# Zeroing cut to 256 rows an expert, loads and reloads spread out, and the turns of retiring tiles queued a unit later

## Chip, cores and metric

One Trainium2 chip, all 8 cores, each running the same program on its own quarter of one of two sequences. The time is device microseconds of the slowest core. Engines: PE is TensorE, DVE VectorE, ACT ScalarE, POOL GpSimd, SP the engine that only issues DMAs. POOL's DMAs go through a software queue (q0), SP's through a hardware queue (q1), on the same 16 DMA engines.

## What is computed

The reference, cut to what matters (x is 2 x 8192 x 1024, f32; b is zero):

```
q, k, v = split(layernorm(x) @ W + b)
x = x + softmax(mask(q @ k.T / 32)) @ v              # causal, one head of 1024
y = layernorm(x); probs = softmax(y @ router_w)       # 8 experts
topw, topi = top_k(probs, 2)
routed = sum over the 2 experts of topw * (silu(y @ w1[e]) @ w2[e])
shared = sigmoid(y @ gate_w) * ((silu(y @ g) * (y @ u)) @ shared_down)
out = x + routed + shared
```

A core computes 2048 query rows (16 tiles of 128 rows) of its sequence against all 8192 keys and values that are not masked away, and then the experts for its 2048 tokens.

## The kernel before, in words

**Attention.** Q's and K's projections are folded into one matrix M. Own tiles are turned (transposed) and multiplied by M into QT, two tiles by one `project(p)`. The keys come in 8 blocks (kb) of 8 tiles of 128 rows; a tile is loaded (POOL), normed (DVE and ACT) to XN and turned by a DMA of SP to XT. The work goes by **units** x = (kb, t), own tile t against key block kb: 72 of them, 16 in block 0, then 14, 12, 10, 8, 6, 4, 2. The loop over x (line 887) issues for each unit: `qk(x)` (PE, L579), `av(x - 2)` (PE, L642, evicted by DVE at L653 or L655), a `project` if x is in `project_at` (line 854), `softmax(x)` (DVE reduce L597, ACT exp L609 into P, then SP's turn PT<-P, L626), the steps of retiring tiles, zeroing and loads, and some steps of the norm of the next block. Each engine and each DMA queue runs in the order of issue. So in program order the softmax of a unit comes behind the eviction of av(x - 2) on DVE, and PE can be more than a unit ahead of it. P has three buffers, PT two.

**Norm steps.** `ln_steps` (line 291) makes a list per block: statistics of tile i (`ln_stats`, DVE), norm of tile i - 1 (`ln_norm`, ACT), turn of tile i - 2 (`ln_turn`, SP, L288). The loop takes the next few of the list each unit. Own tiles 4 to 15 go in block 0, nine steps in units 0 and 1 and five in each later one. Key block 1 has its own list, its turns by hand, two in each of units 10 to 13 (line 931). Tiles 0 to 5 of block 1 are all loaded at unit 5 (line 915), V's weights WV in eight pieces in units 10 to 17 (line 908).

**Retiring tiles.** After the last key block of own tile t its O is finished in four steps. `retire_a` (line 684), at unit x0 = its last unit + 3 (18, 20, 23, 25 for tiles 0 to 3): O / sum into a P buffer (ACT, L689) and the turn QT<-P (SP, L691). `retire_b` at x0 + 2: times WV on PE (L703, then the bias, L706), plus x (DVE, L708), layernorm into xf (ACT, L725) and the turn QT<-xf (SP, L728). `retire_c` at x0 + 5: the router's logits (PE, L739) and top 2; tiles 0 to 9 are stored to R in DRAM by POOL, since their place is needed. `retire_d` at x0 + 6: the place of each token in its expert's rows (L782), and two indirect DMAs of POOL that scatter xf's rows to G. In one unit the order is d, c, b, a.

**Zeroing.** G holds CAP = 640 rows for each of 8 experts. Rows that no token takes must be finite, so `zero_part` (line 867) writes zeros to all of them beforehand: 16 parts of 320 rows (640 KB each), 6 before unit 0 and 2 in each of units 3 to 7, each pair behind a wait of POOL for qk of its unit.

**Experts.** A flag (line 963) tells whether an expert has over 640 tokens; then a dense path runs, which these inputs don't take. The other path (from line 1130): per expert the first product (L1160, 128 matmuls of 320 columns, ACT to hT), then five tiles of the second (L1185, 16 matmuls of 512 columns each), each copied by DVE (L1198) to one of three ys buffers and stored to Y by SP (L1200). Between these tiles the next expert's rows, five tiles in one buffer xn, are turned on PE (`turn_rows`, L989), and after the fourth SP loads the rows of the expert after that (`load_rows`, L982). POOL loads w1 and w2 of expert ex + 2 as soon as their buffers are read. After the first product of expert 0 `back` (line 1017) makes SP reload all ten O tiles from R (L1020). At the end the outputs are gathered by rows, the shared expert's last product is added (L1265), and O is stored.

Of the kernel before, what the change touches and what calls it, by code (L numbers as in the profile page):

```python
# [10 lines left out]
ALU = mybir.AluOpType  # L11
AX = mybir.AxisListType
# [6 lines left out]
EPS = 1e-5  # L19
CAP = 640  # L20


# [59 lines left out]
def build_program():  # L82
# [20 lines left out]
    G = dram("G", [7 * CAP + 2048, D], BF16, kind="Internal")  # L103
    R = dram("R", [10 * 128, D], kind="Internal")
    Y = dram("Y", [8 * CAP, D], kind="Internal")
    out = dram("out", [NT * 128, D], kind="ExternalOutput")
# [184 lines left out]
    def ln_steps(jobs):  # L291
        out_ = []
        for i in range(len(jobs) + 2):
            if i < len(jobs):
                out_.append(lambda i=i: ln_stats(jobs[i]))
            if 0 <= i - 1 < len(jobs):
                out_.append(lambda i=i: ln_norm(jobs[i - 1], False))
            if 0 <= i - 2 < len(jobs):
                out_.append(lambda i=i: ln_turn(jobs[i - 2]))
        return out_  # L300
# [383 lines left out]
    def retire_a(t):  # L684
        i = t % 2
        a = DVE.do(lambda e: e.reciprocal(invl[:, i:i + 1], den[:, t:t + 1]), den_tok[t],
                   ret[t - 2]["ab"] if t > 1 else None)
        p = p_next()
        ab = ACT.do(lambda e: e.activation(out=P[p][:], in_=O[t][:], func=AF.Identity, scale=invl[:, i:i + 1]),  # L689
                    a, o_half[t, 0], o_half[t, 1], p_free[p])  # L690
        k = SP.dma(lambda e: e.dma_start_transpose(qt_cols(t), P[p][:]), d_at[i], ab, qk_last[t])  # L691
        p_free[p] = k
        ret[t] = dict(ab=ab, at=k)

    def retire_b(t):
# [31 lines left out]
        rs_free[z] = a  # L727
        xf_turned[t] = SP.dma(lambda e: e.dma_start_transpose(qt_cols(t), xf[f][:]), d_xf[f], a, k)  # L728
        r["xf"] = a
# [121 lines left out]
    for j in range(9):  # L851
        last_steps += [lambda j=j: ln_stats(kv[1, j])] if j < 8 else []
        last_steps += [lambda j=j: ln_norm(kv[1, j - 1], False)] if j > 0 else []
    project_at = [1, 3, 4, 5, 7, 8, 9]
    steps = []
    retire_at = {}
    for t in range(NT):
        x0 = (18, 20, 23, 25)[t] if t < 4 else units.index((t // 2, t)) + 3
        retire_at.setdefault(x0, []).append((retire_a, t))
        retire_at.setdefault(x0 + 2, []).append((retire_b, t))  # L860
        retire_at.setdefault(x0 + 5, []).append((retire_c, t))
        retire_at.setdefault(x0 + 6, []).append((retire_d, t))
# [3 lines left out]

    def zero_part(i):
        zero_tok[0] = POOL.dma(lambda e: e.dma_start(
            out=G[i * CAP // 2:(i + 1) * CAP // 2, :].rearrange("(s p) d -> p s d", p=64),
            in_=zero[0:64, :].unsqueeze(1).broadcast_to([64, CAP // 128, 1024])), d_zero, k_zeroed)  # L870

# [11 lines left out]
    k_taken = [DVE.do(lambda e: e.tensor_copy(taken[:], e640[:]), k_e640)]  # L883
    for i in range(6):
        zero_part(i)
    x = 0
    while x < n_units or x <= max(retire_at):
# [12 lines left out]
        if x < n_units:  # L900
            softmax(x)
        for step, t in sorted(retire_at.get(x, []), key=lambda v: (retire_d, retire_c, retire_b, retire_a).index(v[0])):
            step(t)
        if 3 <= x < 8:
            POOL.wait(qk_tok[x])
            zero_part(2 * x)
            zero_part(2 * x + 1)
        if 10 <= x < 18:
            w = slice((x - 10) * 1024, (x - 9) * 1024)
            k_wv[0] = POOL.dma(lambda e, w=w: e.dma_start(out=WV[:, w], in_=wvh[:, w]), d_wv, proj_done[7])  # L910
        if x == 18:
            xr_free[0] = zero_tok[0]
            POOL.wait(own[3]["turned"])
            load_xr(0)
        if x == 5:
            for j in range(6):
                ln_load(kv[1, j], POOL)
        for fc, g in fillers.get(x, []):
            gate_up(fc, g)
        if x < n_units:  # L920
            if kb == 0:
# [4 lines left out]
                if x >= 7:  # L926
                    for s in last_steps[:5]:
                        s()
                    last_steps = last_steps[5:]
                if 10 <= x < 14:  # L930
                    ln_turn(kv[1, 2 * x - 20])
                    ln_turn(kv[1, 2 * x - 19])
            elif kb < NKB - 1:
# [18 lines left out]
        for fc in {68: [0], 69: [1], 70: [2], 71: [3], 73: [4], 75: [5], 77: [6], 79: [7]}.get(x, []):  # L952
# [6 lines left out]
    wv_done = ret[NT - 1]["wv"]  # L959

    a = DVE.do(lambda e: e.tensor_tensor(out=rk[:], in0=taken[:], in1=e640[:], op=ALU.subtract), k_taken[0], place_tok[0])
    a = DVE.do(lambda e: e.reduce_max(over, rk[:], axis=AX.X), a)
    k_flag = DVE.do(lambda e: e.tensor_scalar(out=flag[:], in0=over, scalar1=float(CAP), scalar2=None,
                                              op0=ALU.is_gt), a)
# [51 lines left out]
    n = gu_n[0]  # L1016
    def back(queue, turned, k, d_rb):

        for t in range(10):
            tok = queue.dma(lambda e, t=t: e.dma_start(out=O[t][:], in_=R[t * 128:(t + 1) * 128, :]), d_rb, k, *turned)  # L1020
        return {t: tok for t in range(10)}
# [14 lines left out]
    o_done = {}  # L1036
    o_back = back(DSP, xt_tok, gu_done[7], d_rb)
    DPE.wait(k_dw)
# [111 lines left out]
    for ex in range(8):  # L1150
# [4 lines left out]
        for fc in range(8):  # L1155
# [14 lines left out]
            h_ready.append(sp_free[2 * j])  # L1170
        if ex == 0:
            o_back = back(SSP, xt_tok, k1, d_rb)
        if ex + 2 < 8:
# [4 lines left out]
        for s in range(CAP // 128):  # L1178
# [23 lines left out]
            if ex < 7 and s < 4:  # L1202
# [6 lines left out]
                if s == 3 and ex < 6:  # L1209
                    rows_in = load_rows(SSP, ex + 2, rows_out)  # L1210
        if ex + 2 < 8:
            load_w2(ex + 2, k2)
# [163 lines left out]
```

How the kernel before makes its waits and increments, by code:

```python
    def wait(self, *tokens):  # L38
        for t in tokens:
            if t is None:
                continue
            sem, val = t
            if val <= 0 or self.passed.get(id(sem), 0) >= val:
                continue
            self.passed[id(sem)] = val
            self.q.append(lambda e, s=sem, v=val: e.wait_ge(s, v))
# [1 line left out]
    def do(self, fn, *tokens):  # L48
        self.wait(*tokens)
        self.n += 1
        self.q.append(lambda e, f=fn, s=self.sem: f(e).then_inc(s, 1))
        return (self.sem, self.n)
# [5 lines left out]
    def dma(self, fn, slot, *tokens):  # L58
        self.wait(*tokens)
        slot.n += 16
        self.q.append(lambda e, f=fn, s=slot.sem: f(e).then_inc(s, 16))
        return (slot.sem, slot.n)
# [1218 lines left out]
    def run(e, main, one, other):  # L1281
        for fn in main.q:
            fn(e)
        full = e.alloc_register("full")
        e.wait_ge(*k_flag)
        e.reg_load(full, flag[0:1, 0:1])
        with e.If_eq(full, 0):
            for fn in one.q:
                fn(e)
        with e.Else():
            for fn in other.q:
                fn(e)
```

## Time and profile before

| | us |
|---|---|
| median of 3 runs | 1317.23 (1314.55 to 1317.49) |
| the profiled execution | 1328.9 |
| its span, core 7 (the slowest) | 1327.4 |
| spans of the 8 cores | 1293.9 to 1327.4 |
| PE busy on core 7 | 1148.4 (87%) |
| DVE, ACT, POOL busy | 580.6, 463.9, 273.8 |
| granted TensorE clock, mean of core 7 | 0.942 |

The span runs from the first to the last instruction of a core. Busy times are of core 7, and so are all rows below unless said otherwise. PEclk is the granted TensorE clock as a share of 2.4 GHz; at 0.5 a matmul takes twice as long. DMA is the mean busy share of the core's 16 DMA engines. In the name of a line, out<-in are the program's tiles without their numbers; SPq is SP's issue of a DMA, whose own time is that of writing it to the queue, not of the transfer.

### The profile page before, as it was taken

The numbers are of one execution on the slowest core, as the hardware profiler recorded it, in microseconds if no ns is written. First come the engines' busy times: TensorE is split into PE (matmuls) and PEld (weight loads), VectorE is DVE, ScalarE is ACT, GpSimd is POOL, SyncE is SP. The second block draws the span as 40 slices with busy tenths as digits, with TensorE's granted clock in tenths as the row PEclk, the third lists the DMA queues.
The fourth block names the chain that finished last, engine by engine and source line by source line (L and its number), as shares of the span: only waits on it lengthen the run. The fifth ranks groups of instructions, "written<-read, shape, count | busy, mean of one in ns | idle before, by whom it ended". The sixth has DMA issues, their size and how long they took to land.

```text
span 1327.4 us, 18849 instructions; the slowest of 8 cores (1293.9 to 1327.4 us)
## 1 busy us (share of the span) xinstructions
PE 1148.4 (87%) x6360; PEld 583.2 (44%) x6360; DVE 580.6 (44%) x1274; ACT 463.9 (35%) x899; POOL 273.8 (21%) x447
## 2 busy tenths in 40 slices
PE   4888849699989998988876979799985999999897
PEld 1555526244434443433332324344552666665333
DVE  3555315346656665656565654411111111111376
ACT  0344304325443543545445534412321222222200
POOL 4301300101112021221121032350120222111251
PEclk8989969899989999999988979899997999999899
DMA  9987972947766765996959886497398999999687
GB/s 173 242 192 139 212 87 50 149 69 159 131 150 145 167 160 136 203 202 134 187 130 160 154 140 121 77 185 130 102 240 214 198 201 219 223 214 208 236 286 318
DMA packets 249692, 227.03 MB, mean 171 GB/s; under 512 B 186996, under 2 KB 193268, under 8 KB 249592
## 3 DMA queue, kind: packets, MB, share of 16 engines
q0 software_dynamic: 53552, 131.12, 46.2%
q1 hardware_dynamic: 196040, 94.65, 35.5%
q8 instruction: 54, 0.88, 0.3%
q14 instruction: 46, 0.38, 0.1%
HBM read 174.35 MB, written 53.48 MB: 172 GB/s over the span
## 4 chain that ended last, share of the span: by engine, by line
PE 51%; DMA 18%; DVE 11%; ACT 9%; issue 6%; SPq 2%; POOL 1%; another core or an unknown queue 1%; DVEq 0%; ACTq 0%; POOLq 0%
PE po L642 9%; PE po L1185 8%; PE sp L1160 8%; DMA PT<-P 7%; PE sp L827 7%; PE sp L579 6%; PE po L521 4%; PE po L703 4%; DMA xn<-G 3%; DVE per_unit L597 3%; DMA Y<-ys 2%; ACT P L609 2%; PE po L1265 2%; DMA WKT<-wkt 2%; SPq L288 2%
## 5 line engine op out<-in xcount | busy, mean ns | idle before, releaser
L642 PE MATMUL po<-XN,PT 128*128 128x512 bf16 x1064 | 256.8, 397 | 74.9 <-DMA PT<-P 57.0
L579 PE MATMUL sp<-XT,QT 128*128 128x512 bf16 x1064 | 244.5, 383 | 7.1 <-DMA XT<-XN 3.4
L642 PEld LDWEIGHTS po<-XN,PT 128*128 128x128 bf16 x1064 | 106.4, 101 | 217.9 <-issue 107.5
L579 PEld LDWEIGHTS sp<-XT,QT 128*128 128x128 bf16 x1064 | 102.5, 98 | 130.8 <-issue 15.3
L1198 DVE COPY ys<-po 128x1024 f32<-128x1024 f32 x35 | 42.9, 1225 | 239.7 <-PE po L1185 208.6
L827 PE MATMUL sp<-QT,WGU 128*128 128x512 bf16 x512 | 114.3, 383 | 8.4 <-DVE HB L842 8.4
L655 DVE SCALAR_TENSOR_TENSOR O<-O,per_unit,po 128x512 f32<-128x512 f32 x112 | 80.3, 742 | 46.5 <-PE po L642 43.2
L607 ACT ACTIVATE per_unit<-nm,s_q 128x1 f32<-128x1 f32 x72 | 21.2, 295 | 221.4 <-DVE nm L604 88.4
L1167 ACT ACTIVATE hT<-sp 128x640 bf16<-128x640 f32 x64 | 45.0, 703 | 122.4 <-PE sp L1160 110.6
L1185 PE MATMUL po<-SW,hT 128*128 128x512 bf16 x320 | 77.2, 399 | 10.4 <-ACT hT L1167 6.6
L597 DVE TENSOR_REDUCE per_unit<-sp 128x1 f32<-128x1024 f32 (+1 forms) x72 | 83.5, 1160 | 2.0 <-DVE sp L595 0.5
L609 ACT ACTIVATE P<-sp,per_unit 128x1024 bf16<-128x1024 f32 (+1 forms) x72 | 76.7, 1066 | 11.5 <-DMA QT<-P 0.9
L827 PEld LDWEIGHTS sp<-QT,WGU 128*128 128x128 bf16 x512 | 49.9, 99 | 68.5 <-issue 11.4
L703 PE MATMUL po<-WV,QT 128*128 128x512 bf16 x256 | 66.5, 407 | 15.5 <-DVE O L655 8.0
L69 POOL DMA_DIRECT2D xs<-xkv x56 | 30.2, 544 | 217.7 <-ACT XN L278 164.2
L521 PE MATMUL po<-XT,M 128*128 128x256 bf16 x512 | 63.2, 286 | 13.6 <-DVE QT L533 6.6
L1185 PE MATMUL po<-W,hT 128*128 128x512 bf16 x320 | 72.3, 379 | 0.0
L1160 PE MATMUL sp<-xt,W 128*128 128x320 bf16 x512 | 70.4, 299 | 1.5 <-ACT xt L994 1.5
L994 ACT ACTIVATE xt<-sp 128x1024 bf16<-128x1024 bf16 x35 | 35.0, 1022 | 102.3 <-PE sp L989 102.3
L1160 PE MATMUL sp<-xt,SW 128*128 128x320 bf16 x512 | 70.2, 299 | 0.0
L521 PEld LDWEIGHTS po<-XT,M 128*128 128x128 bf16 x512 | 52.0, 102 | 25.3 <-issue 15.7
L69 POOL DMA_DIRECT2D O<-xkv x68 | 36.8, 551 | 113.0 <-ACT mvr L263 56.8
(160 smaller groups left out, 1385.4 us busy)
## 6 DMA issues: line engine op xcount, KB each, us to landing
Y<-ys SPq DMA_DIRECT2D x40, 512.0 KB, 8.0
O<-xkv POOLq DMA_DIRECT2D x68, 256.0 KB, 8.5
xs<-xkv POOLq DMA_DIRECT2D x56, 256.0 KB
G<-zero POOLq DMA_DIRECT2D x16, 640.0 KB, 14.9
xn<-G SPq DMA_DIRECT2D x8, 1280.0 KB, 18.6
xr<-xkv POOLq DMA_DIRECT2D x16, 512.0 KB, 5.0
W<-w1p POOLq DMA_DIRECT2D x32, 256.0 KB, 14.3
W<-w2p POOLq DMA_DIRECT2D x32, 256.0 KB, 17.7
```

Source lines behind the costliest of these rows:

```text
L69: k = queue.dma(lambda e, i=i: e.dma_start(out=out[:, i * w:(i + 1) * w], in_=src[:, i * v:(i + 1) * v]), slot, *tokens)
L521: fn = lambda e, d1=d1, d2=d2, i=i: e.matmul(ring[i][:, 0:256], M[:, d1 * 1024 + d2 * 128:d1 * 1024 + d2 * 128 + 128], rhs(d1), start=(d1 ...
L579: fn = lambda e, d=d, h=h: e.matmul(sp[j][:, h * 512:h * 512 + 512], QT[:, d * 2048 + t * 128:d * 2048 + t * 128 + 128], xt_of(kb)[:, h * ...
L597: a = DVE.do(lambda e: e.reduce_max(lb[:, z:z + 1], sp[j][:, 0:n], axis=AX.X, negate=True), a)
L609: exp_tok[x] = ACT.do(lambda e: e.activation(out=P[p][:, 0:n], in_=sp[j][:, 0:n], func=AF.Exp, bias=ebias[:, z:z + 1], accum_out=lsum[:, z ...
L642: fn = lambda e, c=c, h=h, i=i: e.matmul(ring[i], PT[p][:, c * 128:c * 128 + 128], xn_at(kb, c)[:, h * 512:h * 512 + 512], start=(c == 0), ...
L655: ring_free[i] = DVE.do(lambda e, i=i, dst=dst: e.scalar_tensor_tensor(out=dst, in0=dst, scalar=corr[:, z:z + 1], in1=ring[i], op0=ALU.mul ...
L703: PE.quiet(lambda e, d=d, h=h, b=b: e.matmul(ring[b], QT[:, d * 2048 + t * 128:d * 2048 + t * 128 + 128], WV[:, d * 1024 + h * 512:d * 102 ...
L827: fn = lambda e, d=d, part=part: e.matmul(sp[j][:, part * 512:part * 512 + 512], WGU[fc][:, d * 256 + part * 128:d * 256 + part * 128 + 12 ...
L1160: fn = lambda e, d=d, h=h, fc=fc, i=i, j=j, xt_=xt_: e.matmul(sp[j][:, h * 512:h * 512 + H], SW1[i][:, d * 1024 + fc * 128:d * 1024 + fc * ...
L1167: sp_free[2 * j] = sp_free[2 * j + 1] = SACT.do(lambda e, fc=fc, j=j: e.activation(out=hT[:, fc * CAP:(fc + 1) * CAP].rearrange("p (h n) - ...
L1185: fn = lambda e, fc=fc, h=h, s=s, i=i, j=j: e.matmul(po[j][:, h * 512:h * 512 + 512], hT[:, fc * CAP + s * 128:fc * CAP + s * 128 + 128], ...
```

## The change

1. Zeroing: each expert's rows 384 to 639 only (MIN = 384), one part of 512 KB per expert: four before unit 0, one in each of units 5 to 8. Experts with under 384 tokens would leave rows unwritten, so the flag now sends them, too, to the dense path: it takes the largest (tokens - 512)^2 over the experts and compares it with 128^2.
2. Block 1's tiles 0 to 5 are loaded one in each of units 3 to 8, each behind POOL's wait for that unit's qk; WV in units 9 to 16; block 1's turns in units 9 to 15, one a unit but for two in unit 10.
3. Projections 2, 5, 6 and 7 run one unit earlier.
4. `ln_steps`: the turn of tile i - 3 instead of i - 2, for own tiles and key blocks 2 to 7.
5. Tiles 0 to 13: QT<-P is issued a unit after retire_a and QT<-xf a unit after retire_b; in such a unit the order is turn_a, d, c, turn_b, b, a, all behind PT<-P of the unit. retire_b and retire_c stay where they were. Tiles 14 and 15 keep their order.
6. The ten reloads from R go out in pairs at the end of experts 1 to 5 instead of all in expert 0.

```diff
 CAP = 640
+MIN = 384
...
         out_ = []
-        for i in range(len(jobs) + 2):
+        for i in range(len(jobs) + 3):
...
                 out_.append(lambda i=i: ln_norm(jobs[i - 1], False))
-            if 0 <= i - 2 < len(jobs):
-                out_.append(lambda i=i: ln_turn(jobs[i - 2]))
+            if 0 <= i - 3 < len(jobs):
+                out_.append(lambda i=i: ln_turn(jobs[i - 3]))
...
                     a, o_half[t, 0], o_half[t, 1], p_free[p])
-        k = SP.dma(lambda e: e.dma_start_transpose(qt_cols(t), P[p][:]), d_at[i], ab, qk_last[t])
-        p_free[p] = k
-        ret[t] = dict(ab=ab, at=k)
+        ret[t] = dict(ab=ab, p=p)
...
+    def turn_a(t):
+        p = ret[t]["p"]
+        ret[t]["at"] = p_free[p] = SP.dma(lambda e: e.dma_start_transpose(qt_cols(t), P[p][:]), d_at[t % 2],
+                                          ret[t]["ab"], qk_last[t])
...
+    def turn_b(t):
+        xf_turned[t] = SP.dma(lambda e: e.dma_start_transpose(qt_cols(t), xf[t % 2][:]), d_xf[t % 2],
+                              ret[t]["xf"], ret[t]["wv"])
...
         rs_free[z] = a
-        xf_turned[t] = SP.dma(lambda e: e.dma_start_transpose(qt_cols(t), xf[f][:]), d_xf[f], a, k)
...
         last_steps += [lambda j=j: ln_norm(kv[1, j - 1], False)] if j > 0 else []
-    project_at = [1, 3, 4, 5, 7, 8, 9]
+    project_at = [1, 2, 4, 5, 6, 7, 8]
...
         retire_at.setdefault(x0, []).append((retire_a, t))
+        late = 1 if t < 14 else 0
+        retire_at.setdefault(x0 + late, []).append((turn_a, t))
         retire_at.setdefault(x0 + 2, []).append((retire_b, t))
+        retire_at.setdefault(x0 + 2 + late, []).append((turn_b, t))
...
-    def zero_part(i):
+    def zero_part(ex):
...
         zero_tok[0] = POOL.dma(lambda e: e.dma_start(
-            out=G[i * CAP // 2:(i + 1) * CAP // 2, :].rearrange("(s p) d -> p s d", p=64),
-            in_=zero[0:64, :].unsqueeze(1).broadcast_to([64, CAP // 128, 1024])), d_zero, k_zeroed)
+            out=G[ex * CAP + MIN:(ex + 1) * CAP, :].rearrange("(s p) d -> p s d", p=128),
+            in_=zero[:].unsqueeze(1).broadcast_to([128, (CAP - MIN) // 128, 1024])), d_zero, k_zeroed)
...
     k_taken = [DVE.do(lambda e: e.tensor_copy(taken[:], e640[:]), k_e640)]
-    for i in range(6):
-        zero_part(i)
+    for ex in range(4):
+        zero_part(ex)
...
             softmax(x)
-        for step, t in sorted(retire_at.get(x, []), key=lambda v: (retire_d, retire_c, retire_b, retire_a).index(v[0])):
+        for step, t in sorted(retire_at.get(x, []), key=lambda v: (turn_a, retire_d, retire_c, turn_b, retire_b, retire_a).index(v[0]) if v[1] < 14 else (retire_d, retire_c, retire_b, turn_b, retire_a, turn_a).index(v[0])):
             step(t)
-        if 3 <= x < 8:
+        if 3 <= x < 9:
             POOL.wait(qk_tok[x])
-            zero_part(2 * x)
-            zero_part(2 * x + 1)
-        if 10 <= x < 18:
-            w = slice((x - 10) * 1024, (x - 9) * 1024)
+            ln_load(kv[1, x - 3], POOL)
+        if 5 <= x < 9:
+            zero_part(x - 1)
+        if 9 <= x < 17:
+            w = slice((x - 9) * 1024, (x - 8) * 1024)
...
             load_xr(0)
-        if x == 5:
-            for j in range(6):
-                ln_load(kv[1, j], POOL)
...
                     last_steps = last_steps[5:]
-                if 10 <= x < 14:
-                    ln_turn(kv[1, 2 * x - 20])
-                    ln_turn(kv[1, 2 * x - 19])
+                for j in {9: [0], 10: [1, 2], 11: [3], 12: [4], 13: [5], 14: [6], 15: [7]}.get(x, []):
+                    ln_turn(kv[1, j])
...
     a = DVE.do(lambda e: e.tensor_tensor(out=rk[:], in0=taken[:], in1=e640[:], op=ALU.subtract), k_taken[0], place_tok[0])
-    a = DVE.do(lambda e: e.reduce_max(over, rk[:], axis=AX.X), a)
-    k_flag = DVE.do(lambda e: e.tensor_scalar(out=flag[:], in0=over, scalar1=float(CAP), scalar2=None,
+    a = DVE.do(lambda e: e.tensor_scalar(out=rk[:], in0=rk[:], scalar1=float(CAP + MIN) / -2.0, scalar2=None,
+                                         op0=ALU.add), a)
+    a = DVE.do(lambda e: e.tensor_tensor(out=rk1[:], in0=rk[:], in1=rk[:], op=ALU.mult), a)
+    a = DVE.do(lambda e: e.reduce_max(over, rk1[:], axis=AX.X), a)
+    k_flag = DVE.do(lambda e: e.tensor_scalar(out=flag[:], in0=over, scalar1=float(CAP - MIN) ** 2 / 4.0, scalar2=None,
...
     n = gu_n[0]
-    def back(queue, turned, k, d_rb):
...
-        for t in range(10):
+    def back(queue, tiles, turned, k, d_rb):
...
+        for t in tiles:
...
     o_done = {}
-    o_back = back(DSP, xt_tok, gu_done[7], d_rb)
+    o_back = back(DSP, range(10), xt_tok, gu_done[7], d_rb)
...
             h_ready.append(sp_free[2 * j])
-        if ex == 0:
-            o_back = back(SSP, xt_tok, k1, d_rb)
...
                     rows_in = load_rows(SSP, ex + 2, rows_out)
+        if 1 <= ex < 6:
+            o_back = back(SSP, (2 * ex - 2, 2 * ex - 1), (), k2, d_rb)
```

## Rows read from the trace of the kernel before

**Rows 1.** Waits of PE over the span: who <- releaser: us in total, times, longest.

```profile
PE po L642 <- DMA PT<-P: 57.0, 13, 24.0
...
PE sp L989 <- DMA xn<-G: 14.1, 2, 13.7
...
PE po L703 <- DVE O L655: 8.0, 4, 4.8
```

**Rows 2.** Windows: us, busy (instructions) of PE, PEld, DVE, ACT, POOL; PEclk, DMA, GB/s.

```profile
140.00:190.00 50.00, 26.01 (x160) 14.76 (x159) 10.07 (x21) 9.83 (x20) 10.32 (x18) 0.76 1.03 179
...
400.00:500.00 100.00, 96.02 (x470) 42.97 (x468) 66.85 (x189) 47.40 (x113) 19.51 (x30) 1.00 0.69 158
...
1010.00:1200.00 190.00, 187.74 (x1247) 114.50 (x1248) 30.03 (x25) 53.16 (x65) 39.74 (x76) 0.98 1.01 208
```

**Rows 3.** Timeline, SP's and PE's: start, us, what, [idle before <- releaser].

```profile
135.66 3.62 PE L579 MATMUL sp<-XT,QT 128*128 128x512 bf16 x16
...
140.64 15.74 SPq L288 DMA_TRANSPOSE XT<-XN  x2
...
149.95 3.61 PE L579 MATMUL sp<-XT,QT 128*128 128x512 bf16 x16
...
156.53 13.63 SPq L626 DMA_TRANSPOSE PT<-P  x1
...
184.46 5.39 PE L642 MATMUL po<-XN,PT 128*128 128x512 bf16 x16 [23.99 <-DMA PT<-P]
```

**Rows 4.** DMA queues and one issue group from 140 to 184.5 us.

```profile
q0 software_dynamic: 2016, 7.08, 66.3%
...
G<-zero POOLq DMA_DIRECT2D x6, 640.0 KB, 14.4
```

**Rows 5.** Timeline of PE at unit 13.

```profile
264.52 6.31 PE L642 MATMUL po<-XN,PT 128*128 128x512 bf16 x16 [11.21 <-DMA PT<-P]
```

**Rows 6.** Timeline at retire_b of tiles 0, 2 and 13: next PT<-P, then L703.

```profile
315.98 1.22 SPq L626 DMA_TRANSPOSE PT<-P  x1
317.41 1.46 PE L703 MATMUL po<-WV,QT 128*128 128x512 bf16 x6
...
359.43 1.22 SPq L626 DMA_TRANSPOSE PT<-P  x1
360.18 1.02 PE L703 MATMUL po<-WV,QT 128*128 128x512 bf16 x4
...
785.58 1.22 SPq L626 DMA_TRANSPOSE PT<-P  x1
792.18 1.03 PE L703 MATMUL po<-WV,QT 128*128 128x512 bf16 x4
```

**Rows 7.** Issue to landing: of the turns of L691, and median of all XT<-XN.

```profile
DMA to landing us min/median/max: 3.1/4.0/16.1
...
XT<-XN SPq DMA_TRANSPOSE x60, 6.1
```

**Rows 8.** Timeline of PE, second half of retire_b of tile 3.

```profile
387.17 3.57 PE L703 MATMUL po<-WV,QT 128*128 128x512 bf16 x8 [4.78 <-DVE O L655]
```

**Rows 9.** Timeline of PE at unit 61, second half of qk.

```profile
665.70 3.36 PE L579 MATMUL sp<-XT,QT 128*128 128x512 bf16 x8 [3.43 <-DMA XT<-XN]
```

**Rows 10.** Timeline of experts 0 and 1: issue of the rows, and PE's turn of them.

```profile
993.24 0.76 SPq L982 DMA_DIRECT2D xn<-G  x1
...
1011.83 1.86 PE L989 MATMUL sp<-ident,xn 128*128 128x128 bf16 x16 [13.68 <-DMA xn<-G]
```

**Rows 11.** First products of experts 1, 2 and 3: one timeline row, two of the chain.

```profile
971.54 17.55 PE L1160 MATMUL sp<-xt,SW 128*128 128x320 bf16 x128
...
1030.80 17.39 PE sp L1160 x128
...
1067.69 17.39 PE sp L1160 x128
```

**Rows 12.** DMA issues from 1048 to 1085 us: KB each, median us to landing.

```profile
xn<-G SPq DMA_DIRECT2D x1, 1280.0 KB, 18.7
```


## The prediction

> **What bounds the kernel now.** I read the waits of TensorE first, then the windows by stage, then the timeline at each long wait, and last the DMA issues there. TensorE is the busiest engine, so only its idle time can be won. On core 7 its largest wait is for the turned probabilities, PT<-P: 57.0 us in 13 waits, of which one is 24.0 us; the next is for the gathered rows, xn<-G [rows 1]. The windows show where the two lie: from 140 to 190 us TensorE is busy 26.01 of 50 us while the DMA engines are full, and at full DMA engines from 1010 to 1200 us it is nearly always busy [rows 2]. So three places matter: the first key block, the retiring tiles of 300 to 800 us (many small waits), and the start of the experts.
>
> The sum is made against core 7's profiled execution (1328.9 us, span 1327.4), which is 0.9% above the median of 1317.23; the terms are differences, so I take them off the median.
>
> **Zeroing and loads (first block).** At unit 7 the turn of P of unit 5 is issued at 156.53 and TensorE gets its result at 184.46, after 23.99 us idle, and then runs 16 matmuls in 5.39 us where another 16, in the same rows, take 3.62 at full clock [rows 3]. SP needs 15.74 us to issue two turns of XN and 13.63 us for this one: its ring does not drain. Behind that stand ten half-expert zeroings from unit 3 on and six tile loads at unit 5, all together; in 44.5 us the software queue holds 66.3% of the engines, six zeroings of 640 KB among it [rows 4]. The change writes 8 x 256 rows instead of 8 x 640, four now at the start, and from unit 5 to 8 one zeroing (0.5 MB) and one load (0.5 MB) a unit. At the price of rows 4 (29.5 us of engines for 7.08 MB, 4.2 us/MB) that is 4.4 us a unit; with up to four turns of 1.8 to 2.8 us (the hardware queue's share over its turns) 12 to 15 us, in units that last 14.3 us with their projection (135.66 to 149.95). A turn has over 7 us of slack there, so the wait should go: 24.0 + 1.9 for the clock = **-26**; if a third stays, -17.
>
> Row first, rule second: the turn of a P took 27.5 us with large packets of zeroing and loads beside it [rows 3, 4]. The Trainium skill (DMA: Bandwidth & Descriptors, Queues, rings and completion order) says that each DMA engine goes round its queues packet by packet, so a turn's small packets crawl as long as any large ones are queued. By that rule each unit's burst of 1 MB would still delay a turn, by about its own 4.4 us. That stays under the slack.
>
> **Projections and turns of own tiles.** project(2) moves from unit 3 to 2, and the turn of own tile 5, which it needs, from unit 0 to unit 1, behind PT<-P of unit 1. TensorE would wait some 6 us there (the median of such a turn's landing, rows 7), in place of 4.4 us that it waits for VectorE at project(2) now: **+1** (0 to 5). WV loads start a unit earlier but six of eight still go out in one burst once the last XN is normed, as the seven do now before the wait of 11.21 us [rows 5]; one turn of XT a unit instead of two helps a little: **-1** (-11 to +3).
>
> **Turns of retiring tiles.** This is the part that costs. retire_a's turn QT<-P of tile t is now issued one unit later, behind PT<-P of that unit, but retire_b still uses it on TensorE two units after retire_a. TensorE runs ahead of the softmax: it reaches retire_b of tile 2 at 360.18, when PT<-P of the unit before has only just been issued (359.43) [rows 6]. The turn would follow 1.3 us later and land 4.0 us after its issue [rows 7]: 359.43 + 5.3 = 364.7, 4.6 us late. The same subtraction for the 14 tiles concerned (first and last in rows 6) gives 3.9, 2.8, 4.6, 5.7, 4.2, 0.6, 2.7, 0, 5.0, 0, 5.0, 4.6, 0, 0: 39 us on core 7. The zeros are second tiles of a pair, for which the first's matmuls leave time. TensorE sets the pace here, so a wait mostly stays. Off go 8.0 us in which the same matmuls wait for VectorE anyway [rows 1], and I take 5 off the other small PT<-P waits, for which VectorE catches up. On goes the clock: after 4.78 us idle eight matmuls took 3.57 us [rows 8], against 1.8 (half of 3.62) at full clock: 1.75 us a stall for eight stalls, 14, less some 6 that stalls already there pay: 8. Sum 39 - 8 - 5 + 8 = **+34**. Lower end +10 (VectorE's lag takes up nearly all), upper end 39 + 14 = +53.
>
> Moving QT<-xf (retire_b's turn) costs nothing: retire_c needs it three units later and av of the same unit, ahead of retire_c, waits for a PT<-P issued just before it. It gains once: in unit 58 SP waits for xf of tile 9 before it can issue the last three XT turns, and TensorE then waits 3.43 us and runs at half clock (8 matmuls in 3.36 us) [rows 9]. With that turn gone to unit 59 two of the three go out some 4 us earlier: **-5** (0 to -7).
>
> **Reloading R.** After expert 0's first half SP issues ten 512 KB loads, and every store of Y and the next rows stand behind them: the rows are issued at 993.24 and TensorE gets them at 1011.83 [rows 10]. Expert 1 lasts from 971.54 to 1030.80, 59.3 us; the next cycle, 1030.80 to 1067.69, lasts 36.9 [rows 11]. So 22.4 us on core 7 hang on these loads (the same subtraction gives 19.7 to 27.6 on the other cores). Now two follow each of experts 1 to 5: **-22**. Back comes what 1 MB more costs a cycle of 36.9 us that moves 7.7 MB (208 GB/s) on full engines [rows 2]: nothing if the slack takes it, 5.2 MB at 208 GB/s = 25 us if all is on the path. The nearest deadline is xn<-G: it lands 18.7 us after its issue [rows 12] and is needed about 23 us after it (a tile of 3.9, less the copy, 17.4 of the next first half, 3.5). The new loads are behind it in SP's ring, so **+2**.
>
> The Trainium skill (DMA: Bandwidth & Descriptors, Specifications) gives about 358 GB/s of HBM per core. By the f32 weights (8.4 MB), rows, stores and the new loads, a cycle would move 13.4 MB, 37.3 us by that figure instead of 36.9: +2 us over five experts, as an estimate; no row shows the limit itself.
>
> Sum: -26 + 1 - 1 + 34 - 5 - 22 + 2 = -17, so **1300**. A measurement of this kernel can't tell less than about 0.3% (4 us) from no change.
>
> **Rivals.**
> - *The late turns are absorbed* (term +10): 1276. For it: VectorE is the late one at tile 3 [rows 8], and a delayed TensorE finds fewer such waits. Against: from 400 to 500 us VectorE is busy 67 of 100 us and TensorE 96 [rows 2]. Chance 0.22.
> - *The late turns cost more than all else gives; slower.* Place: L703 of the nine late tiles. Right behind another turn, XT<-XN lands a median of 6.1 us after issue, not 4.0 [rows 7]: 2 us more for nine tiles, and every stall at half clock after it: 39 + 14 + 18 = 71, less some 5: +66, giving 1332. It decides from 55 us, 6 us a tile. For it: the turn is always behind a PT<-P now. Against: SP issues them 1.2 us apart, and XT's median includes crowded stages. Chance 0.15.
> - *The experts become DMA-bound* by the spread loads: xn<-G over 23 us, some 3 us an expert, +15: 1313. For it: engines at 1.01. Against: weights are asked for 55 us ahead. Chance 0.12.
> - *The first block's wait stays in part*, as loads and zeroing still start with the unit's scores: +9, 1309. Chance 0.03.
> - The branch to the dense path now also opens under 384 tokens an expert. The reference's routing of these inputs gives 438 to 573 on every core, so no chance is kept for it.
>
> **How the numbers follow.** The forecast keeps 0.48, own range 1286 to 1314. The absorbed case's middle bounds the range below, 1276; above, 1325 leaves out about half of the slower rival and more. Faster: 0.45 of the forecast, 0.22, 0.06 of the third, 0.02 of the fourth = 0.75; slower: 0.15 and 0.02; 0.08 between.
>
> **What would show it.** In the profile after: no wait over 5 us for PT<-P before 200 us, with full clock; a wait near 10 us at 215 to 240 us; a new row L703 <- DMA QT<-P with nine or ten waits of 3 to 6 us, 25 us or more in all, none for the second tiles of pairs; no wait for XT<-XN near 640 us; expert 1 in some 37 us, xn<-G landing under 23 us. I am wrong if QT<-P waits stay under 10 us (then the first rival), or if waits of L1160, L1185 or L989 return in every expert.

## The result: slower, and the profile after

The changed kernel took 1348.05 us (median of 4 runs) beside 1317.36 for the kernel before on the same chip: ratio 1.0225, 95% interval 1.0188 to 1.0262, so 30 us slower where 17 faster was forecast. One of its four runs, 1409.19 us, had the cores of one die at a clock of 0.85 to 0.86 and is left out of the ratio, as such runs are in every ratio below, though not in the medians. Its profiled execution took 1347.06 us, the spans of its cores 1327.7 to 1345.5. Lines below L291 have moved: L579 is now L580, L642 L643, L655 L656, L691 L698, L703 L713, L1160 L1174, L1185 L1197, L1231 L1245. The rows are of core 7, as ahead of the prediction. First four of TensorE's waits over the span of the profile after (us in total, times, longest):

```profile
PE po L713 <- DMA QT<-P: 38.1, 8, 6.4
...
PE po L643 <- DVE O L656: 15.6, 5, 5.1
PE po L643 <- DMA PT<-P: 14.5, 8, 6.1
...
PE po L713 <- DVE O L656: 5.3, 2, 4.9
```

Against [rows 1], the wait for PT<-P has gone from 57.0 to 14.5 us and that for xn<-G is out of the list, as forecast, and QT<-P has come in with 38.1. The windows, same columns as [rows 2]:

```profile
140.00:190.00 50.00, 50.00 (x375) 32.87 (x372) 22.37 (x46) 18.12 (x40) 6.11 (x11) 1.00 0.62 111
...
400.00:500.00 100.00, 88.48 (x422) 39.00 (x420) 60.71 (x161) 44.40 (x104) 19.01 (x29) 0.96 0.64 146
1010.00:1200.00 190.00, 185.42 (x1237) 112.56 (x1236) 30.62 (x25) 53.21 (x65) 44.76 (x85) 0.99 1.04 225
```

The first block is cured: TensorE busy 50 of 50 us at full clock instead of 26.01 at 0.76. Between 400 and 500 us it has lost 7.5 us of busy time, and no row of one wait shows all of it. So I cut the span at five marks on TensorE, taken from the first and last starts of its lines, and give the mean over the 8 cores of the profiled execution. "Experts' products" runs from the first to the last start of the experts' first products, "rest" from there to the end. The table holds the later runs too; each row is one execution, and the runs were made on several chips, so differences of a few us between rows are weak:

| kernel | to the first retire_b product | retire_b, first to last | to expert 0 | experts' products | rest | mean span |
|---|---|---|---|---|---|---|
| before | 316.2 | 494.6 | 108.8 | 300.1 | 88.6 | 1308.2 |
| after | 299.9 | 543.6 | 108.8 | 286.0 | 96.5 | 1334.7 |
| e1_turns_back | 296.9 | 523.1 | 108.9 | 286.5 | 97.1 | 1312.4 |
| e2_only_b_late | 295.3 | 521.4 | 108.5 | 286.9 | 96.4 | 1308.6 |
| e3_reload_back | 300.0 | 546.4 | 108.4 | 300.3 | 90.7 | 1345.9 |
| e5_chain_later | 301.7 | 507.3 | 109.0 | 287.7 | 96.3 | 1302.2 |
| e8_e1_steps2 | 292.2 | 491.4 | 108.5 | 285.8 | 95.3 | 1273.4 |
| e9_e1_late_turns_old_slots | 291.3 | 492.9 | 108.7 | 284.5 | 96.7 | 1274.1 |
| e10_after_steps2 | 295.8 | 520.1 | 109.0 | 285.0 | 94.7 | 1304.5 |
| e11_e5_steps2 | 299.2 | 486.9 | 108.9 | 285.5 | 95.6 | 1276.2 |
| e6_before_first_block | 291.0 | 488.7 | 109.0 | 300.9 | 89.9 | 1279.5 |
| e13_before_steps3 | 318.9 | 518.9 | 109.0 | 300.1 | 90.4 | 1337.2 |
| e12_e8_no_reload | 291.2 | 489.8 | 108.5 | 277.4 | 92.9 | 1259.6 |
| e14_e8_y_bf16 | 289.6 | 490.2 | 108.9 | 275.8 | 84.1 | 1248.5 |

The loss is in one stretch: retiring, +49 us, against 29 forecast there (+34 for the late turns, -5 for an XT turn). The experts gave 14 of the 22 us hoped for, and the rest of the span took 8 back.

### The profile page after: what moved, and what is told of

It is laid out like the page before. It is cut to its first block, busy times and chain, and to the rows that moved or that the text cites. A ratio compares the mean times of both kernels' runs of the same rounds, so it can differ in the third digit from the quotient of the medians.

```text
span 1345.5 us, 18797 instructions; the slowest of 8 cores (1327.7 to 1345.5 us)
## 1 busy us (share of the span) xinstructions
PE 1158.1 (86%) x6360; PEld 585.1 (43%) x6360; DVE 580.1 (43%) x1276; ACT 465.6 (35%) x899; POOL 266.7 (20%) x439
## 4 chain that ended last, share of the span: by engine, by line
PE 50%; DVE 15%; DMA 13%; ACT 11%; issue 7%; SPq 2%; POOL 1%; another core or an unknown queue 1%; DVEq 0%; ACTq 0%; POOLq 0%
PE po L1197 9%; PE sp L1174 9%; PE po L643 7%; PE sp L836 6%; PE sp L580 5%; PE po L522 4%; PE po L713 4%; DVE per_unit L598 3%; DMA gb<-Y,lohi 3%; ACT P L610 3%; PE po L1279 2%; DMA QT<-P 2%; DVE O L656 2%; DMA PT<-P 2%; DMA WKT<-wkt 2%
## 5 line engine op out<-in xcount | busy, mean ns | idle before, releaser
L643 PE MATMUL po<-XN,PT 128*128 128x512 bf16 x1064 | 254.3, 393 | 37.6 <-DMA PT<-P 19.3
L580 PE MATMUL sp<-XT,QT 128*128 128x512 bf16 x1064 | 244.9, 383 | 15.1 <-ACT P L610 9.2
L643 PEld LDWEIGHTS po<-XN,PT 128*128 128x128 bf16 x1064 | 105.9, 101 | 177.2 <-issue 64.1
L580 PEld LDWEIGHTS sp<-XT,QT 128*128 128x128 bf16 x1064 | 102.3, 98 | 139.5 <-issue 24.6
L713 PE MATMUL po<-WV,QT 128*128 128x512 bf16 x256 | 77.6, 457 | 56.5 <-DMA QT<-P 36.9
L656 DVE SCALAR_TENSOR_TENSOR O<-O,per_unit,po 128x512 f32<-128x512 f32 x112 | 79.9, 740 | 38.8 <-PE po L643 34.6
L1197 PE MATMUL po<-W,hT 128*128 128x512 bf16 x320 | 73.9, 385 | 5.9 <-DMA W<-w2p 5.9
L1174 PE MATMUL sp<-xt,W 128*128 128x320 bf16 x512 | 70.4, 299 | 4.1 <-DMA W<-w1p 2.6
L713 PEld LDWEIGHTS po<-WV,QT 128*128 128x128 bf16 x256 | 27.9, 113 | 101.2 <-issue 83.9
L1197 PE MATMUL po<-SW,hT 128*128 128x512 bf16 x320 | 71.7, 379 | 0.0
L1279 PE MATMUL po<-W,HB 128*128 128x512 bf16 x256 | 60.3, 400 | 12.3 <-DVE O L1286 12.3
L1174 PE MATMUL sp<-xt,SW 128*128 128x320 bf16 x512 | 70.2, 299 | 0.0
```

The source lines that it names most:

```text
L580: fn = lambda e, d=d, h=h: e.matmul(sp[j][:, h * 512:h * 512 + 512], QT[:, d * 2048 + t * 128:d * 2048 + t * 128 + 128], xt_of(kb)[:, h * ...
L643: fn = lambda e, c=c, h=h, i=i: e.matmul(ring[i], PT[p][:, c * 128:c * 128 + 128], xn_at(kb, c)[:, h * 512:h * 512 + 512], start=(c == 0), ...
L656: ring_free[i] = DVE.do(lambda e, i=i, dst=dst: e.scalar_tensor_tensor(out=dst, in0=dst, scalar=corr[:, z:z + 1], in1=ring[i], op0=ALU.mul ...
L713: PE.quiet(lambda e, d=d, h=h, b=b: e.matmul(ring[b], QT[:, d * 2048 + t * 128:d * 2048 + t * 128 + 128], WV[:, d * 1024 + h * 512:d * 102 ...
L1174: fn = lambda e, d=d, h=h, fc=fc, i=i, j=j, xt_=xt_: e.matmul(sp[j][:, h * 512:h * 512 + H], SW1[i][:, d * 1024 + fc * 128:d * 1024 + fc * ...
L1197: fn = lambda e, fc=fc, h=h, s=s, i=i, j=j: e.matmul(po[j][:, h * 512:h * 512 + 512], hT[:, fc * CAP + s * 128:fc * CAP + s * 128 + 128], ...
```

## The experiments

Every ratio is to the kernel before, run beside each of these on the same chip.

### First four: undo one part of the change

**e1_turns_back**: the turns of retiring tiles as before.

```diff
-        late = 1 if t < 14 else 0
+        late = 0
...
-        for step, t in sorted(retire_at.get(x, []), key=lambda v: (turn_a, retire_d, retire_c, turn_b, retire_b, retire_a).index(v[0]) if v[1] < 14 else (retire_d, retire_c, retire_b, turn_b, retire_a, turn_a).index(v[0])):
+        for step, t in sorted(retire_at.get(x, []), key=lambda v: (retire_d, retire_c, retire_b, turn_b, retire_a, turn_a).index(v[0])):
```

> Edit: the changed kernel with both retiring turns issued in their old units and the old order in a unit (late = 0); all else of the change stays. Theory A (the late QT<-P costs what retire_b waits for it): the stretch from the first L713 to the last falls from about 544 us to about 494 us as before the change, the waits L713 <- DMA QT<-P from 37 to 44 us a core to under 5 us, and the time to 1298 us (1292 to 1304). Theory B (the reloads and the spread loads cost, and the turns little): under 15 us back, 1335 us or more. Theory C (half of the loss in that stretch comes from the norm's turns one job later): the stretch stays at 515 us or more, about 1320 us.

**e2_only_b_late**: as e1, but QT<-xf stays a unit late (`turn_a` at x0, `turn_b` at x0 + 2 + late).

> Edit: the changed kernel with QT<-P issued at once, behind retire_a, and only QT<-xf a unit late. Theory A (deadline of QT<-P alone): as the run with both turns back, 1298 us, or up to 4 us less if QT<-xf out of the way of the norm's turns helps at the end of block 4. Rival D (QT<-xf late is the dearer, by retire_c or by holding the xf buffers): 1325 us or more with waits of L748 on QT<-xf.

**e3_reload_back**: all ten reloads in expert 0 again.

```diff
+        if ex == 0:
+            o_back = back(SSP, range(10), xt_tok, k1, d_rb)
...
-        if 1 <= ex < 6:
-            o_back = back(SSP, (2 * ex - 2, 2 * ex - 1), (), k2, d_rb)
```

> Edit: the changed kernel with the ten reloads from R all in expert 0, as before the change. If spreading them gains what the prediction said (20 us net), 1368 us. If its gain is given back later (weights of experts 5 to 7 late, gathers late at the end), as the profile after suggests (experts 14 us shorter, the end 9 us longer), 1353 us (1349 to 1358), with waits of L1174 and L1197 for weights gone and the end (first L1279 to end) back at about 70 us.

**e5_chain_later**: turns late as in the change, and retire_b, turn_b, c and d of tiles 0 to 11 a unit later too, so that a turn has its two units again.

```diff
-        retire_at.setdefault(x0 + 2, []).append((retire_b, t))
...
+        more = 1 if t < 12 else 0
+        retire_at.setdefault(x0 + 2 + more, []).append((retire_b, t))
...
```

> Edit: the changed kernel, with retire_b, QT<-xf, retire_c and retire_d also one unit later for tiles 0 to 11, so that QT<-P has its old distance to its reader. Theory A (a deadline): most of the 50 us come back, waits L713 <- DMA QT<-P under 12 us a core (tiles 12 and 13 keep theirs), 1303 us (1296 to 1312). Rival E (the turn itself collides: behind PT<-P it takes 6.5 us instead of 4 and holds its P buffer, whoever reads it): waits of ACT L610 and PT<-P stay, 1330 us or more.

Measured: e1 1320.06 us, ratio 1.0005 (0.998 to 1.0031); e2 1317.95, 0.9976 (0.9932 to 1.002); e3 1357.97, 1.0265 (1.0224 to 1.0307); e5 1313.96, 0.995 (0.9923 to 0.9977).

What follows. The late QT<-P is real: without it the retiring stretch is 20.5 us shorter (e1), and giving it its unit back by other means cuts its waits to at most 7.6 us a core (e5). The late QT<-xf costs nothing (e2 is 2.1 us below e1), as forecast. But theory A fell with e1: with the late turns gone the kernel should have been near 1298 and was at 1320, its retiring stretch still 28.5 us longer than before; e2 and e5, expected at 1298 and 1303, came out above it too, at 1317.95 and 1313.96. Theory C had e1's numbers (515 us or more, about 1320) and laid them to the norm's turns coming late, which the next runs put right. What stands there in the waits of core 7 of e1 is

```profile
PE po L713 <- DVE O L656: 27.3, 8, 5.3
```

where the kernel before has 8.0 in 4 [rows 1]: TensorE waits for VectorE's eviction of O, and VectorE in turn waits for the root that ScalarE takes for the norm, in the same run and then in the kernel before:

```profile
DVE mvr L267 <- ACT mvr L264: 114.6, 72, 4.5
```

```profile
DVE mvr L266 <- ACT mvr L263: 91.7, 69, 4.0
```

Of the change's items only one touches VectorE's order in that stretch: `ln_steps`, with its turn at i - 3 instead of i - 2. I had read it as a turn a slot later.

### Second four: the list of norm steps

**e8_e1_steps2**: e1 with the list as before.

```diff
-        for i in range(len(jobs) + 3):
+        for i in range(len(jobs) + 2):
...
-            if 0 <= i - 3 < len(jobs):
-                out_.append(lambda i=i: ln_turn(jobs[i - 3]))
+            if 0 <= i - 2 < len(jobs):
+                out_.append(lambda i=i: ln_turn(jobs[i - 2]))
```

> The kernel after, with the late turns taken back (as in the run with only those undone) and the list of norm steps of the next blocks as before too: statistics, norm and turn of a tile in slots i, i-1 and i-2 instead of i, i-1 and i-3. The retiring stretch (first to last retire_b product) took 523.1 us without the late turns, and 494.6 us in the kernel before. Theory F: the extra slot shifts the list against the units, so that VectorE meets the norm, which waits for ScalarE's root, before the statistics instead of after them, stands idle and evicts retire_b's product late; with the slot gone the stretch returns to 493 to 500 us and the time to 1291 to 1297 (ratio to the kernel before 0.976 to 0.983), and the waits of L713 for the eviction of O fall from about 27 us to about 10. Rival G: the 28 us come from the other changed places that last (the projections, the WV loads and the spacing of the first block leave the later stretches a unit earlier, or chip to chip difference): then the time stays at 1316 to 1322.

**e9_e1_late_turns_old_slots**: the same, but each entry of a turn issues the turn of the tile before (the first issues none, the last two), so turns are late and the list isn't shifted.

```diff
-            if 0 <= i - 2 < len(jobs):
-                out_.append(lambda i=i: ln_turn(jobs[i - 2]))
+            if 2 <= i <= len(jobs) + 1:
+                out_.append(lambda i=i: [ln_turn(jobs[k]) for k in ([i - 3] if i > 2 else []) + ([i - 2] if i == len(jobs) + 1 else [])])
```

> As the run before it, but each turn of XN is issued one slot later without a slot of its own: the list keeps the length and the order of the kernel before, and only the DMA of the turn moves. Theory F (the order of norm and statistics on VectorE costs, not the turns): within 4 us of the run with the old list, 1290 to 1299. Rival G (the later turns of XN themselves cost, since they land late beside other turns or hold XN's buffer): 1310 to 1322, with waits of the scores for XT<-XN over 15 us.

**e10_after_steps2**: the kernel after with e8's list and nothing else.

> The kernel after with the old list of norm steps alone; the late turns stay. Theory F with additive terms: the retiring stretch 543.6 - 28 = 515 us, time 1318 to 1324 (ratio to the kernel before about 1.00). If late turns and list overlap (both only make TensorE wait for the same thing), less: 1300 to 1312, or more than 1330 if the late turns cost their full 39 us once nothing else is late.

**e11_e5_steps2**: e5 with e8's list.

> The late turns with the steps b, c and d of a tile a unit later too (so that the turn has its two units again), and the old list of norm steps. With the new list this took 1314 (retiring stretch 507.3 us). Theory F: the stretch falls to 480 to 487 us and the time to 1285 to 1292, the fastest of all. Rival: once b is a unit later the eviction's lateness no longer costs, and the list gives 10 us or less: 1304 to 1314.

Measured: e8 1293.37 us, 0.9758 (0.9679 to 0.9836); e9 1288.73, 0.9712 (0.9628 to 0.9796); e10 1319.57, 0.9945 (0.9903 to 0.9987); e11 1289.81, 0.9757 (0.968 to 0.9835).

The old list gives 2.5% without the late turns (1.0005 to 0.9758), 2.8% with them (1.0225 to 0.9945) and 1.9% in e5 (0.995 to 0.9757). It is the places in the list that cost, not the lateness of XT's turns: e9, with late turns and old places, is as fast as e8. In e8 the waits of core 7 read

```profile
DVE mvr L267 <- ACT mvr L264: 92.1, 69, 4.0
...
PE po L713 <- DVE O L656: 6.5, 4, 3.1
```

and in e10, where the late QT<-P is left alone, they are, for TensorE,

```profile
PE po L643 <- DMA PT<-P: 27.9, 11, 12.5
PE po L713 <- DMA QT<-P: 24.1, 6, 8.0
```

The late turns cost 23.5 us of mean span up to the last retire_b with the new list (after less e1) and 32.3 with the old (e10 less e8). By the ratios it is 2.2% and 1.9%, the other way round, so the runs don't tell whether late turns and list overlap.

### Last four: each cause by itself

**e13_before_steps3**: the kernel before with the list of the change alone (the reverse of e8's diff).

> The kernel before with nothing but the extra slot in the list of norm steps (turn in slot i-3, not i-2). Theory F, the order of norm and statistics on VectorE: the retiring stretch 493 -> 515 to 525 us and the ratio 1.017 to 1.027. Rival: the slot costs only beside the change's other parts (the first block's single turns, the units moved), and alone it is within 0.5% of no change.

Measured: 1349.77 us, ratio 1.0253 (1.0205 to 1.0302). This one edit makes the kernel before as slow as the whole change made it.

The trace shows how. A unit takes the next entries of a list of 24, three each in the block of units 42 to 51. Written out as statistics S, norm N, turn T with the tile's number, both lists have the same length; only the cuts fall elsewhere:

```
before: S0 S1 N0 | S2 N1 T0 | S3 N2 T1 | S4 N3 T2 | S5 N4 T3 | S6 N5 T4 ...
after:  S0 S1 N0 | S2 N1 S3 | N2 T0 S4 | N3 T1 S5 | N4 T2 S6 | N5 T3 S7 ...
```

The statistics now stand in a unit behind a norm, and tiles share staging buffers: tiles 0, 4 and 6 the first, 1, 5 and 7 the second. S6 right behind N4, and S7 behind N5, read the buffer that this norm has just freed, and its load hasn't even started. VectorE of core 1 of the kernel before, between the retire_b products of tiles 6 and 7 (start, us, what, [idle before <- releaser]):

```profile
553.95 0.21 DVE L266 TENSOR_SCALAR mvr<-mvr 128x1 f32<-128x1 f32 x1 [0.79 <-ACT mvr L263]
554.08 0.68 DVE L257 BATCH_NORM_STATS2 st<-xs 128x6 f32<-128x512 f32 x1
...
556.20 0.21 DVE L266 TENSOR_SCALAR mvr<-mvr 128x1 f32<-128x1 f32 x1 [0.53 <-ACT mvr L263]
556.33 0.74 DVE L655 SCALAR_TENSOR_TENSOR O<-O,per_unit,po 128x512 f32<-128x512 f32 x1
```

and VectorE, POOL and TensorE of core 1 of e13 at the same place:

```profile
551.21 0.21 DVE L266 TENSOR_SCALAR mvr<-mvr 128x1 f32<-128x1 f32 x1 [2.03 <-ACT mvr L263]
...
553.31 1.06 POOL L69 DMA_DIRECT2D xs<-xkv  x2 [4.49 <-ACT XN L278]
...
558.71 0.69 DVE L257 BATCH_NORM_STATS2 st<-xs 128x6 f32<-128x512 f32 x1 [7.29 <-DMA xs<-xkv]
...
560.23 1.38 DVE L655 SCALAR_TENSOR_TENSOR O<-O,per_unit,po 128x512 f32<-128x512 f32 x2
...
561.09 3.57 PE L703 MATMUL po<-WV,QT 128*128 128x512 bf16 x8 [6.36 <-DVE O L655]
```

Before, the statistics stand ahead of the norm (S5 at 554.08, then N4 at 556.20) and the eviction of av's product, O L655, follows at once. In e13 the norm N4 comes first, behind 2.03 us of waiting in place of 0.53, ScalarE reads the buffer, POOL issues the next load at 553.31, and the statistics wait 7.29 us for it. In-order VectorE holds the eviction of O behind them; TensorE stands for 6.36 us and then runs eight matmuls at half clock, 3.57 us instead of 1.89. That is one kind. The other is the norm's own wait for ScalarE's root, which the statistics no longer cover. Over the span of this core the waits read before

```profile
DVE mvr L266 <- ACT mvr L263: 90.9, 69, 4.0
...
PE po L703 <- DVE O L655: 11.0, 6, 3.1
```

and in e13

```profile
DVE mvr L266 <- ACT mvr L263: 114.6, 72, 4.5
...
PE po L703 <- DVE O L655: 27.0, 8, 6.4
```

VectorE's waits for xs<-xkv go from 8.8 us to 20.0. On TensorE both kinds end in the second row: 16 us more, and some 7 more by the clock (the groups of eight matmuls behind these waits take in all 9.3 us over 1.89 each, and 2.7 before). That is 23 of the 24.9 us by which this core's stretch grew. How the loss divides between the two kinds wasn't separated.

**e6_before_first_block**: items 1 to 3 of the change (zeroing, loads and WV, projections) put into the kernel before.

> The kernel before with the first block's change alone: half-size zeroing and its spacing, one XN load a unit, the WV loads and projections earlier, the single turns of XN; turns of retiring tiles, norm list and reload as before. By the stages of the runs so far (end of the last projection 35 us sooner, of which some 10 come back because one more unit lies behind it) the theory gives -25 us, ratio 0.979 to 0.984, and retiring and expert stages as before within 4 us. Rival: what the first block gives is partly the reload's or lost later, then 0.988 or more.

Measured: 1292.58 us, 0.9821 (0.9782 to 0.986), 24 us faster. Its mean span is 28.7 us shorter: 25.2 us of it come before the first retire_b product, 6 in the retiring stretch.

**e12_e8_no_reload**: VectorE sets tiles 0 to 9 of O to zero in place of the reload. It leaves the attention's part out of these tiles.

```diff
-            o_back = back(SSP, (2 * ex - 2, 2 * ex - 1), (), k2, d_rb)
+            for t in (2 * ex - 2, 2 * ex - 1):
+                o_back[t] = SDVE.do(lambda e, t=t: e.memset(O[t][:], 0.0), k2)
```

> The kernel after without late turns and without the extra slot (1293 us), and with O of tiles 0 to 9 set to zero by VectorE in place of its reload from R: it leaves the attention's part out of these ten tiles. If the stage of experts and end (first expert product to the end of the span, 380 us) is bound by the bytes that its DMAs move, 5.2 MB less give 15 to 25 us: stage 355 to 365, time 1268 to 1278. Rival: spread out, the reload is hidden already, and what waits at the end waits for the gathers' own latency: 376 to 380 us, 1288 to 1293.

**e14_e8_y_bf16**: Y, its staging ys and the gathered gb in bf16 (their three declarations changed from F32).

> The same kernel (1293 us) with the experts' results Y kept in bf16 in place of f32, in their staging, in memory and in the gathers: 10.5 MB less stored and 8.4 MB less gathered. It changes the rounding of the experts' part. Theory of a stage bound by its bytes: the waits of L1245 for gb<-Y (about 44 us) fall below 10 us, the last stretch (78 us) to 55 to 60, expert stage down 5 to 15 more, time 1262 to 1275. Rival, the gathers are bound by their row descriptors (2048 rows of 2 KB in place of 4 KB) and not by bytes: the last stretch stays above 72 us and the time above 1282.

Measured: e12 1270.2 us, 0.9651 (0.9622 to 0.968); e14 1264.29, 0.9596 (0.9563 to 0.9629). So the spread reload isn't hidden: from the first expert product to the end 370.3 us in e12 and 381.1 in e8, 11 less, where 15 to 25 were expected by bytes. e14 is 21 less than e8 there (359.9) and within its range of time, but by other shares than I wrote: the last stretch, from the first product of the shared part on, went from 77.9 to 65.3 us where 55 to 60 was expected, and the experts gave 10. VectorE's waits for the gathers, core 7 of e3, after and e14 in that order:

```profile
DVE O L1245 <- DMA gb<-Y,lohi: 20.4, 7, 14.4
```

```profile
DVE O L1245 <- DMA gb<-Y,lohi: 44.5, 13, 34.0
```

```profile
DVE O L1245 <- DMA gb<-Y,lohi: 11.7, 3, 10.9
```

With the reload in expert 0 the gathers are waited for 20.4 us, with the spread reload 44.5; core 7 is the extreme, the means of the eight cores are 25.6 and 40.6. It would be easy to say that the same 5.2 MB, moved later, meet the gathers. But e12, which reloads nothing, still has, on core 7,

```profile
DVE O L1246 <- DMA gb<-Y,lohi: 39.2, 15, 23.6
```

and 34.9 us in the mean. So most of this rise doesn't need the reload's bytes; that the rest of the traffic has less time once the stall in expert 1 is gone is likely, but wasn't tested. Where the reload does stand in the way is one step earlier, at the late experts' weights: TensorE waits for them 7.1 us a core in the kernel after (3.8 to 10.3), and not at all before, in e3 and in e12 (timeline of core 7, as [rows 11]):

```profile
1026.74 17.55 PE L1174 MATMUL sp<-xt,W 128*128 128x320 bf16 x128
...
1063.63 17.55 PE L1174 MATMUL sp<-xt,SW 128*128 128x320 bf16 x128
...
1196.90 4.90 PE L1197 MATMUL po<-W,hT 128*128 128x512 bf16 x16 [3.76 <-DMA W<-w2p]
```

Experts 2 and 3 lie 36.89 us apart; the cycle of expert 6 has a wait for w2p in it. In e12 and e14 TensorE has no wait for a weight on any core, and their experts' products take 277.4 and 275.8 us.

## Why the prediction was wrong

In the order of its terms:

- **Zeroing and loads, -26, with +1 and -1 beside it.** Right: e6 gives 24 us by its ratio, 25.2 up to the first retire_b product. No wait over 5 us for PT<-P before 200 us and full clock, as stated; the wait forecast at 215 to 240 us came as 6.05 us at 240.31 on core 7. On core 5 SP needs 10.22 us there to issue one turn, with seven pieces of WV and four halves of tile loads issued by POOL in the 9 us around it, and TensorE waits 12.83:

```profile
223.09 10.22 SPq L627 DMA_TRANSPOSE PT<-P  x1
242.87 6.27 PE L643 MATMUL po<-XN,PT 128*128 128x512 bf16 x16 [12.83 <-DMA PT<-P]
```

- **Late turns, +34.** Right, and the subtraction tile by tile held: waits of L713 for QT<-P of 38.1 us in 8 against the 39 in ten worked out, one of them 0.6; in mean span 32.3 us with the old list, 23.5 with the new. Tiles 0, 3, 4, 6, 8, 10 and 11 wait 4.26, 4.25, 6.38, 3.39, 6.01, 3.53 and 4.27 us (forecast 3.9, 5.7, 4.2, 2.7, 5.0, 5.0 and 4.6). Tile 2 waits 6.50 and tile 1 2.18 under VectorE's name (forecast 4.6 and 2.8). Tile 12 waits 6.00 where 0 was forecast. That 0 was misread: the zeros were called second tiles of a pair, and 12 is a first one, whose product at 784.40 in the kernel before stood behind a wait of 4.58 us for its own QT<-P. Tile 4's:

```profile
438.75 1.22 SPq L627 DMA_TRANSPOSE PT<-P  x1
440.01 1.30 SPq L698 DMA_TRANSPOSE QT<-P  x1
...
443.73 3.57 PE L713 MATMUL po<-WV,QT 128*128 128x512 bf16 x8 [6.38 <-DMA QT<-P]
```

  The turn goes out 1.26 us behind PT<-P, lands 3.7 us later, and TensorE has stood for 6.38. The landing of these turns, a median of 3.4 us on core 7 (3.1 to 5.9), speaks against the rival that made the change slower by a landing of 6.1.
- **The list of norm steps (item 4), no term; XT turns, -5.** This is the step that failed. Item 4 stood in the change as a turn that moves by a slot, and the sum has no term for it and no reason for leaving it out; all that it prices of these turns is XT's own reader at unit 61. It is a list that the unit loop deals out by count, so one entry moved re-cuts all that follow it, and the entries are VectorE's and ScalarE's work. Neither the forecast nor a rival has VectorE's order in it. By e13 it costs 2.5% alone, some 33 us; by mean spans 23 to 36 up to the last retire_b, in four pairs of kernels (e13 less before, e1 less e8, after less e10, e5 less e11). The 3.43 us at unit 61 [rows 9] did shrink, to a wait of 1.16, and don't matter beside it.
- **Reload, -22 + 2.** The mechanism was right, the size of what comes back was not. Expert 1 took 36.9 us and its wait for xn<-G is gone, but the stage from the first expert product to the end gave 8.5 us (after against e3), 9.7 (e8 against e6). I looked for the nearest deadline, the rows of the next expert, and took 2 us. The debt came due at the later ones: the weights of the late experts (7.1 us a core), and a longer wait of VectorE for the gathers at the end (25.6 to 40.6 us in the mean), some 6 of which reach the span (rest: 96.5 against 90.7). The "25 us if all is on the path" stood in the working as the far bound; the sum should have taken some 13.

With these two terms as measured the prediction's own sum is -26 + 1 - 1 + 34 - 5 - 22 + 13, that is -6, and the list's 23 to 36 on top: +17 to +30, against 30 measured. By mean spans the chain before, e6, e8, e10, after reads -28.7, -6.1, +31.1, +30.2, which sum to the 26.5 by which the mean span grew: first block, reload, late turns, list. That slower had 0.17 was no foresight, since the rival that held most of it had its price from the landing of the turns, and that was not what happened. Neither of the two signs that were to show the forecast wrong appeared either: both watched terms that had a price.

The rule of the Trainium skill beside the first term (DMA: Bandwidth & Descriptors, Queues, rings and completion order), that each DMA engine goes round its queues packet by packet, agrees with core 5's 10.22 us issue; that a turn crawls as long as large packets are queued was the prediction's own step from it, and the same issue bears it out. The other figure that the Trainium skill gives (DMA: Bandwidth & Descriptors, Specifications), about 358 GB/s of HBM for a core, is not shown as a limit by any run. TensorE set the cycle, which stayed at 36.89 us with 1 MB more in it. From 1026.7 to 1100.7 us core 7 of the kernel after landed 16.90 MB, 6.85 of them weights counted at their bf16 size; with these read as f32 that is 23.8 MB, an estimate of 321 GB/s. The windows' GB/s count weights in the same small way and can't be set beside the 13.4 MB.

## What to carry to other kernels

When steps are dealt out to slots by count, an entry moved in the list moves all behind it against the slots: write the sequence of each in-order engine for a few units before and after, and look for an operation that now stands right behind the one that frees its buffer. A transfer moved off a wait isn't gone where the DMA engines are full; follow it to the last deadline of that stage, and bound it by leaving it out, which also shows what would be late without it. And undo each item of a change alone: here two gave 24 and 5 to 10 us and two took some 25 to 37 each, and the version with only the good ones (e8, 1293.37 us) beats both kernels, as does the same with Y in bf16 (1264.29), which rounds the experts' part more coarsely.

## What was not expected of the hardware

The busy share of the DMA engines doesn't say whether they bind. From 1010 to 1140 us on core 7 the windows of e8 and e14 read (columns as [rows 2])

```profile
1010.00:1140.00 130.00, 124.81 (x837) 77.26 (x836) 18.37 (x15) 36.15 (x45) 28.05 (x53) 0.99 1.03 224
```

```profile
1010.00:1140.00 130.00, 130.00 (x889) 80.98 (x887) 18.98 (x16) 37.83 (x48) 29.59 (x57) 1.00 1.06 207
```

Both are at 1.03 or more, the second with 17 GB/s less and TensorE never idle. What tells them apart is who waits: in the first TensorE 5.2 us for w1 and VectorE 3.1 us for the stores of Y, in the second nobody for a DMA.
